# The output bias added by VectorE behind a chunk's last square, in place of GpSimd

## The reference

```
xn  = layernorm(x)
out = x + attn(xn) + ffn(xn)

attn: proj = xn @ in_w + in_b                     # v and two controls, 256 wide each
      for i in 0, 1:
          v = fft_conv(v, filter_i)               # long causal convolution over the sequence
          v = v * gated_control_i                 # 3-tap convolution, sigmoid gate
      return v @ out_proj_w + out_proj_b          # the output bias of this case
ffn:  h = bitlinear(xn, w_fc) + gate * (xn @ v.T @ fast_b.T @ u.T)
      r = max(h, 0)
      return bitlinear(r * r, w_proj)             # ternary weights and a scale per channel
```

## Time and profile before

| | us |
|---|---|
| median of 3 runs | 882.59 |
| lowest and highest run | 881.22, 882.63 |
| profiled execution, its own time | 882.74 |
| its span | 880.8 |
| PE busy | 837.3 (95%) |
| DVE busy | 621.8 (71%) |
| ACT busy | 471.4 (54%) |
| POOL busy | 238.6 (27%) |

### The profile page before, as it was taken

The page is one execution under the profiler, slowest core; times in us unless marked ns, Lnnn a source line. Parts: engine busy times, 40 slices in busy tenths (PEclk is TensorE's granted clock), DMA queues, the critical chain, the costliest instruction groups (busy, mean ns, idle before and its releaser), DMA issues.

```text
span 880.8 us, 25943 instructions
## 1 busy us (share of the span) xinstructions
PE 837.3 (95%) x9920; PEld 695.4 (79%) x9921; DVE 621.8 (71%) x1041; ACT 471.4 (54%) x698; POOL 238.6 (27%) x248
## 2 busy tenths in 40 slices
PE   8779999999999997999999999999999999999997
PEld 3468888888888866878888888777887787788997
DVE  7849988988999884565665566566546656666887
ACT  6757777787877763444435353434444444444221
POOL 4445646655664402021112112111011201200000
PEclk9989999999999999999999999999999999999999
DMA  8762243234323268768767778677887876952896
GB/s 217 235 217 97 96 149 138 95 103 162 116 95 138 102 165 242 156 138 196 173 162 156 189 167 197 124 168 181 181 151 171 180 174 115 202 111 47 221 314 209
DMA packets 90687, 142.03 MB, mean 161 GB/s; under 512 B 12861, under 2 KB 70606, under 8 KB 89742
## 3 DMA queue, kind: packets, MB, share of 16 engines
q1 hardware_dynamic: 72990, 101.80, 48.7%
q0 software_dynamic: 7728, 28.05, 10.0%
q10 hardware_dynamic: 9920, 11.54, 4.0%
HBM read 97.39 MB, written 43.97 MB: 160 GB/s over the span
## 4 chain that ended last, share of the span: by engine, by line
PE 47%; DVE 9%; issue 4%; ACT 1%; DMA 1%; DVEq 0%; POOL 0%; ACTq 0%; POOLq 0%
PE pp L1372 13%; PE py L1391 13%; PE pf L1341 11%; DVE r L1163 3%; PE pf L1347 3%; PE py L1428 2%; PE py L1359 2%; DVE pp L1153 2%; DVE r_lo L1168 1%; DVE GC L1158 1%; DVE xb L1158 1%; PE pp L457 1%; PE pp L459 1%; PE pp L458 1%; ACT r_hi L1275 1%
## 5 line engine op out<-in xcount | busy, mean ns | idle before, releaser
L1275 ACT ACTIVATE r_hi<-r 128x512 fp32r<-128x512 f32 x128 | 80.9, 632 | 149.4 <-DVE r L1163 149.4
L1391 PEld LDWEIGHTS py<-vwin,lead 64*64 64x64 f32 x5120 | 132.9, 133 | 25.2 <-issue 25.2
L1372 PE MATMUL pp<-wproj,r_hi 128*128 128x256 f32 x512 | 135.3, 297 | 14.6 <-DVE r_lo L1168 10.4
L1270 ACT ACTIVATE r<-pf,fscale 128x512 f32<-128x512 f32 x128 | 87.8, 686 | 111.5 <-PE pf L1347 111.4
L1391 PE MATMUL py<-vwin,lead 64*64 64x128 f32 (+4 forms) x5120 | 146.9, 265 | 0.5 <-issue 0.5
L1168 DVE TENSOR_TENSOR r_lo<-r,r_hi 128x512 fp32r<-128x512 f32 x128 | 93.1, 727 | 67.2 <-ACT r_hi L1275 67.1
L1341 PE MATMUL pf<-tokens,split_a 128*128 (+1 forms) x512 | 139.6, 394 | 0.9 <-issue 0.9
L1372 PE MATMUL pp<-wproj,r_lo 128*128 128x256 f32 x512 | 126.7, 281 | 0.0
L1372 PEld LDWEIGHTS pp<-wproj,r_hi 128*128 128x128 f32 x512 | 96.1, 188 | 32.1 <-DVE r_lo L1168 14.3
L498 POOL TENSOR_SCALAR lead<-lead,norms 128x256 f32<-128x256 f32 x64 | 117.8, 1851 | 3.4 <-POOL norms L492 3.4
L660 DVE SCALAR_TENSOR_TENSOR xc<-ctrl,taps,xc 128x512 f32<-128x512 f32 x128 | 96.8, 776 | 18.8 <-ACT xc L766 18.1
(11 more groups left out here) (189 smaller groups left out, 1531.1 us busy)
## 6 DMA issues: line engine op xcount, KB each, us to landing
lead<-filters SPq DMA_DIRECT2D x128, 320.0 KB, 6.2
xnT_hbm<-split_b SPq DMA_DIRECT2D x32, 512.0 KB, 3.3
tokens<-xnT_hbm POOLq DMA_DIRECT2D x30, 512.0 KB, 5.1
lead<-in_attn_x SPq DMA_DIRECT2D x16, 512.0 KB, 4.1
gc_hbm<-xc SPq DMA_DIRECT2D x16, 512.0 KB, 2.6
GC<-gc_hbm SPq DMA_DIRECT2D x32, 256.0 KB, 6.3
out<-GC ACTq DMA_DIRECT2D x15, 512.0 KB, 6.4
GC<-in_attn_x POOLq DMA_DIRECT2D x9, 512.0 KB, 7.5
```

Source lines behind the costliest of these rows:

```text
L1270: act.activation(r[j][:, :], pf[:, j, :], ACT.Relu, scale=fscale[:, m:m + 1]).then_inc(relu_done, 1)
L1275: act.activation(r_hi[j][:, :], r[j][:, :], ACT.Copy).then_inc(r_hi_done, 1)
L1372: last = pe.matmul(pp[:, i, :], part[m % 2][:, i * P:(i + 1) * P], wproj[:, m, :], start=(m == 0 and n == 0 and i % 2 == 0), stop=(m == HT ...
L1391: last = pe.matmul(py[g % 2][q * BW:(q + 1) * BW, side, l, :, A:NB], tile[rows, q * PAIR + l, j * BW:(j + 1) * BW], vwin[g % 2][rows, q, l ...
```

## The change

GpSimd no longer adds the bias. `load_xb` still issues the transfer and waits for it, and then only raises the new semaphore `xb_here`. A new function `biased` on VectorE waits for `bo_row` and for `xb_here`, adds the bias in place, and raises `xb_biased`, for which `add` waits as before. `biased` is called at the end of VectorE's chunk body, behind the square of tile 7. GpSimd's wait for `bo_row` ahead of its first load is gone too. As the buffer to be used changes at the end of the first half, `lagging` with `closing` now writes out the last chunk of both halves.

```
-            end = ITERS - (closing and order == ORDERS - 1)
+            end = ITERS - closing
...
                 pool.dma_start(buf, x_tiles[bass.ds(it, 1)].rearrange("c p i d -> (c p) i d")).then_inc(xb_loaded, 16)
-                wait_alone(pool, xb_loaded, it * 16 + 16, pool_passed)
-                pool.tensor_tensor(buf, buf, bo_row[:, :].unsqueeze(1).broadcast_to([P, TT, D]), ALU.add).then_inc(xb_biased, 1)
+                wait_alone(pool, xb_loaded, it * 16 + 16, xb_here)
...
-            pool.wait_ge(bo_in, 16)
             load_xb(0, True)
...
+            def biased(it, buf):
+                dve.wait_ge(bo_in, 16)
+                dve.wait_ge(xb_here, it + 1)
+                dve.tensor_tensor(buf, buf, bo_row[:, :].unsqueeze(1).broadcast_to([P, TT, D]), ALU.add).then_inc(xb_biased, 1)
...
                     if g < GPI - 1:
                         low(it, 2 * g + 1)
+                if last:
+                    biased(it, sums[KEPT - 1])
+                elif order:
+                    biased(it, kept_sum(m + 1))
+                elif isinstance(m, int) and m == ITERS - 1:
+                    biased(it, kept_sum(0))
+                else:
+                    biased(it, xb[:, :, :])
```

More of the change, by code:

```diff
@@ L959, in mix_stage @@
         pp = ctx.enter_context(nc.psum_tensor("pp", [P, TT, D], F32))
-        bo_in, srow_in = sem("bo_in"), sem("srow_in")
+        bo_in, srow_in, xb_here = sem("bo_in"), sem("srow_in"), sem("xb_here")
         sp_passed, pool_passed, pe_passed = sem("sp_passed"), sem("pool_passed"), sem("pe_passed")
```

## The result

The changed kernel has a median of 873.14 us (870.16 to 873.84, 4 runs) against 882.61 us before (881.22 to 882.9, 4 runs). The ratio is 0.9889, with a 95% interval of 0.9863 to 0.9915. Two later series of five and six runs gave 873.02 and 871.48 us, with ratios to the kernel before of 0.9893 (0.987 to 0.9915) and 0.9876 (0.9852 to 0.99). The forecast was 870.5 us, faster, within 868.8 to 874.0. The kernel before had medians of 881.70 and 881.92 us beside those two. Direction and mechanism came out, and about four fifths of the size: 9.5 us less in the first series, 8.7 and 10.4 in the later ones, where the forecast had 12.1. Over all series the 42 runs of the kernel before have a mean of 881.9 us and the 15 of the changed kernel one of 872.4, 9.5 less as well.

A forecast was written before the change was run, and what follows sets the result against it. TensorE, busy for 95% of the span, was taken as the bound, held up by VectorE's late `r_lo` tiles. 882.74 - 13.2 (holds) + 1.1 (last chunk) = 870.6, forecast as 870.5 us against the median, range 868.8 to 874.0.

The forecast's parts named there:

- The holds: Mixing stage: GpSimd's bias additions delay VectorE's squares, so TensorE waits ten times for `r_lo`; removing them saves 10.4 + 1.9 + 0.2 us.
- The periods of 27.70 us: Mixing stage: a chunk that took 28.83 us with one hold should take 27.70 without it.
- The spread of 0.3 us: Uncertainty given to the sum of the holds within the forecast's range.
- the rule cited there: A two-SBUF-input VectorE instruction competes with a GpSimd instruction reading SBUF; the later waits for the whole of the other.
- The eleventh hold: Convolution block early in the mixing stage: a square of 2.67 us at 385.81 makes the block 0.76 us longer; 0.8 us saved.
- the prediction's slack of 1.24 us: Waits behind a convolution block: about 1.24 us of slack precede them, so a hold costs less there.
- The chunk ends: Fifteen chunk ends: the addition on VectorE fits in 2.25 us of slack, leaving 1.15; cost 0, at most 5 us.
- The last chunk: End of the last chunk: nothing covers the addition on VectorE, so the closing part moves by +1.1 us, at most 2.4.
- A: Chunk ends: GpSimd's transfer issues hold the addition, TensorE loses about 4 us over 8 ends, 874.5 us; chance 0.07.
- B: First groups: half of the 11 holds are replaced by waits of like length, 877 us; chance 0.08.
- C: First half: x's tile lands late and stops VectorE, making the kernel slower, 886 us at 10 us later; chance 0.02.
- D: Mixing stage: the landing of x's tile slows VectorE, so holds stay and only the 1.1 us shows, 883.7; chance 0.03.

The follow-up runs named there:

- the run that brings it back: Changed kernel with GpSimd adding the bias again and VectorE doing a same-size maximum at the new place: 883.1 us, ratio 1.0014 to the kernel before.
- the run that only writes: Changed kernel with three GpSimd zero-fills of half the idle buffer behind each landing of x in chunks 8 to 15: 871.54 us.
- the variant of the kernel before: Kernel before with only the last chunk's bias addition moved to VectorE, the other 15 left on GpSimd: 882.58 us, ratio 1.0015.

## Why the prediction was right

*The holds.* Right in kind, and in size for the execution that was priced. The forecast had ten of them at 10.4 + 1.9 + 0.2 = 12.5 us; start to start the traces give 12.5. The periods of 27.70 us came out to 0.01. But the size changes from one execution to the next: the three traces with GpSimd's additions have nine, ten and eleven such waits of 9.5, 10.4 and 12.6 us (one of the nine-wait trace's 16 additions is on VectorE). The spread of 0.3 us that the prediction gave them was too narrow. That GpSimd's tensor_tensor is the cause is shown by the run that brings it back; that its reading is what matters fits with the run that only writes, and is not shown apart from it.

One number of the prediction's working is off: at 758.20 GpSimd's addition had 758.04 + 2.39 - 758.20 = 2.23 us to go, not 2.27, so by the rule cited there the square would last 2.91 us, and it took 2.77. That is no chance of one row: in seven held squares of three traces the square ends 0.54 to 0.56 us behind GpSimd's addition, a little less than its own 0.68.

*The eleventh hold.* This is the step that failed, the term of 0.8 us. I took the stop inside chunk 1's convolution block for an effect of the held square because that was 1.99 us late just before. But the stop is in kernels without any GpSimd tensor_tensor in this stage too. Its timeline in the changed kernel:

```profile
386.91 2.16 PE L1402 MATMUL py<-vwin,lead 64*64 64x128 f32 x73
390.67 0.42 PE L1402 MATMUL py<-vwin,lead 64*64 64x112 f32 x7 [1.59 <-issue]
```

It stops behind the 73rd of 80 matmuls, the same place as before the change, now for 1.59 us. In the 14 traces of this study its length ranges from none (four of them) to 1.85 us (in the variant of the kernel before). Two more traces of the changed kernel, unedited, have 0.48 and 0.49, as before has 0.46. "Issue" meant what it says: nothing that the profile shows released it. The three traces with the held square have 0.46, 1.04 and 1.85 us, the eleven without it 0 to 1.59, so a share of the hold in it can't be excluded by so few, but the stop doesn't need the hold. The hold did have a price of its own, by the prediction's slack of 1.24 us: 1.99 - 1.24 = 0.75. In this execution it lay hidden behind the stop, for `r_lo` was ready at 389.17 + 0.69 = 389.86 and the first matmul that needs it, behind the stopped block, came at 389.95:

```profile
389.17 0.69 DVE L1168 TENSOR_TENSOR r_lo<-r,r_hi 128x512 fp32r<-128x512 f32 x1 [0.69 <-ACT r_hi L1275]
...
389.95 0.39 PE L1372 MATMUL pp<-wproj,r_hi 128*128 128x256 f32 x1
```

Both ran side by side, and taking one away gives back only what it has over the other. The change from 0.46 us before to 1.59 in the first trace after is scatter between executions, and the change of the kernel can't be credited with it. Without this term the sum is 882.74 - 12.4 + 1.1 = 871.4, and 871.3 by the median.

*The chunk ends.* Right, cost 0. The slack left is 1.35 us in the trace and was 1.15 by the forecast, which took the addition to push `r_lo` back by 1.1 us. It pushed it by 0.90: from the last square's start to `r_lo`'s it is 2.35 us now and was 1.45.

*The last chunk.* Right at 1.1 us: the wait for the last `r_lo` is new, and what follows moves by that. In the second trace of the changed kernel the stretch from the last rank product to the last transposition is just that much longer, 91.4 us against 90.3.

*What was not in the sum.* In the profiled execution the half clock (1.1 us) and the very end (from the last transposition 12.2 us instead of 11.1) add 2.2 us. The end takes 11.1 to 12.7 us over the 14 traces, and the closing clock fell in one of them. The sum had no term for such scatter, only its range did, and the trace of before has a whole clock and the shortest end of all. Without the eleventh hold the sum promises 11.3 us less than before; the means over all runs differ by 9.5, with an interval of about 0.9 to either side. So some 1.8 us of the gain are missing, and these runs don't say where. The profiled execution of before is 0.9 us above the mean of its kernel's 42 runs, so that its holds may have been dearer than usual, and its short end works the other way. A mean's surplus can't be split among such terms, since only one execution of a kernel in each series has a trace. What causes the stop in chunk 1 and the different ends was not settled.

*The rivals.* A (the addition is held by GpSimd's transfers) is refuted by the chunk end above, where both run together at usual length. B (half the gain) did not occur. C (a late tile): no wait of VectorE for `xb_here` appears. D (the landing holds VectorE): landings are where they were, and the squares are short.

## What to carry to other kernels

An engine that is not the bottleneck can still hold the one that is: when an instruction's longest duration is four times its median, look at what GpSimd does at that moment, and at how many operands each of the two reads from SBUF. Price such a hold by its excess minus the slack of the waiting engine, with a place in the same trace where nothing is held as the reference, and add the lost overlap of the restart. Take the sum of such holds from more than one trace, for it changes from one execution to the next. Leave waits that the profile puts down to "issue" out of the sum, unless a second trace shows them the same; and when a queue is reordered, ask what the moved instruction's place was idle for.

## What the runs showed that was not expected

A GpSimd memset of 128 x 512 values takes 0.53 us and runs beside VectorE's squares without changing their 0.68 us, while a GpSimd tensor_tensor of 128 x 1024 stretches one to 2.89 us at most. In chunk 1, the first pass through its loop, TensorE stops behind the 73rd of 80 matmuls of a convolution block, for 0 to 1.85 us from one trace to the next. A wait of 0.64 us for the rank rows was followed by a second stop of about 0.6, although its operand was ready. And the clock was at its lower level for 3.4 us in one execution and whole in two others of the same kernel, and in six of its variants with the same waits ahead; the tile that ran in it took 1.15 us longer.
